# A vision tower on one core: edge products in row groups of 64, two pairs ahead, between the products of Q and K

## The chip, the cores and the metric

One core of a Trainium2 chip runs the whole kernel as one program. The metric is device time in microseconds. Before the change the median of three runs is 305.49 us (305.42 to 306.01).

## The reference, cut to what matters

Eight images of 3 x 256 x 256 go through three stages; the last two have weights of their own.

```python
def tok(x, scharr):                       # x (8, 3, 256, 256)
    gray = einsum('bchw,c->bhw', x, (0.2989, 0.587, 0.114))[:, None]
    edges = conv(gray, scharr, stride 1, 'SAME')          # two 3 x 3 filters
    return abs(edges).sum(axis=1) / 2     # (8, 256, 256): 256 tokens of width 256

def attn(x, Wq, bq, Wk, bk, Wv, bv, Wp):  # 16 heads of 16
    q, k, v = (x @ W + b for W, b in ...)
    q, k = q @ Wp, k @ Wp                 # for each head
    return softmax(q k^T / sqrt(16)) v

def ffn(x, ...):                          # 256 -> 1024 -> 256, weights dequantized
    h = layernorm(x) * gamma + beta
    return x + 0.5 * (silu(h @ w1 + b1) @ w2 + b2)

h = tok(x); h = h + attn(layernorm(h)); h = h + ffn(layernorm(h))
```

## The kernel before

Images are handled as four pairs. Each engine has its own list of instructions, run strictly in the order in which the code issues them; semaphores join them. There are three parts on the time axis: the image part with the products of Q, K and V (to about 100 us of the span), the attention loop (to about 207 us), and the MLP. Matrix products are split in a high and a low part of each operand, so one product of exact size takes three matmuls (`product`, line 1142).

**Image part.** For an image, ScalarE scales the first colour (`gray_scale`), VectorE adds the other two (`gray_add`, lines 724 and 725), ScalarE writes the high part (`gray_high`) and VectorE or GpSimd the low part (`gray_low`). The convolution is done on TensorE with band matrices: for a tile of 128 image rows (`t` is 0 or 1), and each of the two filters (`k`), nine matmuls (three column shifts `dx`, three high and low combinations) with 128 rows of contraction and 512 columns (two images of 256). A tenth (line 1164) adds what comes over the tile's edge, the halo, from 96 stacked rows. That is `tok(p, i)` with `i = 2 * t + k`. ScalarE takes the absolute value of each (line 1024, into `absd` or `hid`), VectorE adds the two (`edges`, line 794), and takes mean and variance (`tok_moments`); GpSimd computes `rstd` (line 543), VectorE normalises (line 813) into `xn`. TensorE transposes `xn` (`xt`), ScalarE and VectorE split it in `xt_h` and `xt_l`. Then come the six products of the pair, `qkv(p, 0)` to `qkv(p, 5)`: two of Q, two of K, one of V for each image. ScalarE (`qk_high`) and VectorE (`qkv_out`, line 838) take the first four out of PSUM, VectorE the last two.

**Order on TensorE** for pair `p`: `tok(p + 1, 0)` and `tok(p + 1, 1)`, the transposes of pair `p`, `tok(p + 1, 2)` and `tok(p + 1, 3)`, then the six products. They share the PSUM banks 4 to 7 by turns. In the last pairs the first ten heads' scores by query (line 1212) are put in between, by the table `HEAD_AT`; VectorE takes their largest value (`largest`, line 848).

**Way over DRAM.** Q and K go to DRAM and come back in another layout, both on SP's queue: `store_qk(p, i)` (line 379, two DMAs) once VectorE has read product `i`, and `load_qk(p, m, k)` (line 389, twelve DMAs for each half `m` of a pair). SP's order is: four stores of pair 0, 24 loads of pair 0, four stores of pair 1; then it waits until all edges are added, since the loads of pair 1 land where the image part has its buffers; twelve loads, the stores of pair 2, twelve loads, the stores of pair 3, and then the weights of the MLP (lines 401 and 404).

**Attention loop.** Slot `s` of 64 handles two heads: scores by query of slot `s + 10`, scores by key of slot `s` (lines 1235 and 1240, on partitions 0 to 47 and 64 to 111, into two banks), the exponential on ScalarE, the product with V (line 1260). In every fourth slot TensorE transposes the split maxima (`neg`, line 1270); for slot 11 that is `neg(2, 0)`. GpSimd's order there is: at slots 6, 7 and 8 the first steps of `w1_step` (dequantizing the MLP's first weights, lines 610 and 613, the first waits for the weights' DMA), at slot 9 `split_max(2, 0)` (lines 553 and 556), which `neg(2, 0)` waits for.

Of the kernel before, what the change touches and what calls it, by code (L numbers as in the profile page):

```python
# [5 lines left out]
def vit_tower_kernel(nc, x, scharr, Wq, bq, Wk, bk, Wv, bv, Wp, ln_gamma, ln_beta,  # L6
# [6 lines left out]
    fp32 = mybir.dt.float32  # L13
# [21 lines left out]
    HALF = P // 2  # L35
    NCOL = HALF + SPLIT
# [39 lines left out]
    halo_m = at("halo_m", 17.9375, [P, NT, 3], fp32)  # L76
    halo_p = at("halo_p", 18, [P, NT, 2, 3], fp32)
    halo_w = at("halo_w", 18.0625, [P, NT * 2], fp32)
    halo_wh = at("halo_wh", 18.125, [P, NT * 2], fp32r)
    halo_wl = at("halo_wl", 18.1875, [P, NT * 2], fp32)  # L80
# [16 lines left out]
    band_h = at("band_h", 83.25, [P, 2, 3, P], fp32r)  # L97
    band_l = at("band_l", 86.25, [P, 2, 3, P], fp32r)
    halo = at("halo", 89.25, [96, B, E], fp32r)
    halo_b = at("halo_b", 97.25, [96, NT, 2, P], fp32r)  # L100
# [11 lines left out]
    masks = at("masks", 141.25, [P, 3, P], fp32)  # L112
# [5 lines left out]
    halo_x = at("halo_x", 143, [32, B, E], fp32)  # L118
# [4 lines left out]
    bandp = at("bandp", 163, [P, 2, 3, P], fp32)  # L123
    band = at("band", 167, [P, 3, P], fp32)
    band1 = at("band1", 173, [P, 3, P], fp32)
# [28 lines left out]
    def norms_of(p):  # L154
        return (xt2_h, xt2_l) if p == PAIRS - 1 else (xt_h, xt_l)
# [6 lines left out]
    with ctx:  # L162
# [9 lines left out]
        s_halo = sem("halo_loaded")  # L172
# [14 lines left out]
        s_bandp = sem("second_band_parts_ready")  # L187
        s_band1 = sem("second_band_ready")
# [6 lines left out]
        s_wready = sem("qkv_weights_ready")  # L195
# [11 lines left out]
        s_fill = [sem(f"filled{r}") for r in range(4)]  # L207
        s_free = [sem(f"freed{r}") for r in range(4)]
# [32 lines left out]
        XT_LAST = (PAIRS - 2, 3)  # L241
        turns = []
        for p in range(-1, PAIRS):
            if p + 1 < PAIRS:
                turns.extend(("tok", p + 1, i) for i in range(2 if p >= 0 else 4))
            if p >= 0:
                if p + 1 < PAIRS:
                    turns.extend(("xt", p, kf) for kf in range(KE))
                    turns.extend(("tok", p + 1, i) for i in (2, 3))
                for i in range(6):  # L250
                    turns.append(("qkv", p, i))
                    if (p, i) == XT_LAST:
                        turns.extend(("xt", p + 1, kf) for kf in range(KE))
        turn = {key: n for n, key in enumerate(turns)}
        last_turns = [[key for key in turns if turn[key] % 4 == r][-1] for r in range(4)]

        def turn_bank(key):
            return bank[4 + turn[key] % 4]

        def wait_filled(eng, key):  # L260
            n = turn[key]
            eng.wait_ge(s_fill[n % 4], n // 4 + 1)

        def wait_freed(eng, key):
            n = turn[key]
            if n >= 4:
                eng.wait_ge(s_free[n % 4], n // 4)

        def wait_read(eng, key):
            n = turn[key]  # L270
            eng.wait_ge(s_free[n % 4], n // 4 + 1)

        def filled(key):
            return s_fill[turn[key] % 4]

        def freed(key):
            return s_free[turn[key] % 4]
# [4 lines left out]
        HEAD_AT = {("tok", 3, 1): 0, ("tok", 3, 3): 1, ("qkv", 2, 0): 2, ("qkv", 2, 2): 3, ("qkv", 2, 3): 4, ("qkv", 2, 5): 5,  # L282
# [74 lines left out]


# [5 lines left out]
        N3_READ = {n + 2: key for n, key in N3_MADE.items()}  # L364

# [3 lines left out]
        def _(eng):  # L369
# [37 lines left out]
            load_x(0)  # L407
            load_x(1)
# [5 lines left out]
            load_x(2)  # L414
            load_x(3)
# [6 lines left out]
            for b in range(4, B):  # L422
                load_x(b)
# [266 lines left out]
        def _(eng):  # L690
# [228 lines left out]
            for op in range(2):  # L919
                weights(op)  # L920
# [516 lines left out]
```

## Time and profile before

| | us |
|---|---|
| median of 3 runs | 305.49 |
| the profiled execution | 305.62 |
| its span | 303.9 |
| TensorE busy, of the span | 291.6 (96%) |
| VectorE busy | 214.6 (71%) |
| ScalarE busy | 161.5 (53%) |
| GpSimd busy | 130.9 (43%) |

The span runs from the first to the last instruction of the profiled execution; what lies around it is 1.7 us here. A busy share is an average over three parts with different limits. TensorE's matmuls overlap (a 512-column one shows 0.40 us, and the next starts 0.23 us later), so the distance between starts is what one costs.

### The profile page before, as it was taken

The page shows a single profiled execution, that of the slowest core. Times are in us where ns is not written, and L with a number is a line of the kernel's source. Part 1 is how long each engine was busy: PE and PEld are TensorE (multiplying, and loading weights), DVE is VectorE, ACT ScalarE, POOL GpSimd, SP SyncE. Part 2 cuts the span into 40 slices and gives each one's busy share as a digit, 9 for nine tenths or more (in the row PEclk, how much of TensorE's full clock was granted, in tenths as well). Part 3 has the DMA queues.
Part 4 walks back from the last instruction along what each step waited for, and adds up shares of the span by engine and source line. Part 5 has one row for each costly group of instructions (what it writes and reads, how often), then busy time and mean ns, then how long its engine had stood idle before and what let it go on. Part 6 is the DMA issues. An engine that isn't in the chain of part 4 may idle for free.

```text
span 303.9 us, 6265 instructions
## 1 busy us (share of the span) xinstructions
PE 291.6 (96%) x2328; PEld 229.6 (76%) x2328; DVE 214.6 (71%) x423; ACT 161.5 (53%) x304; POOL 130.9 (43%) x250
## 2 busy tenths in 40 slices
PE   6799999999999999999999999999999999999996
PEld 6678888887787666666666666667998998989976
DVE  8978994775899988888889887636845724633332
ACT  1492453433333577768776777867345343434550
POOL 7515250421100018862768572156769489500000
PEclk9999999999999999999999999999999999999999
DMA  6968028782497971778573000000000100200202
GB/s 211 327 195 275 1 92 284 208 287 101 125 296 220 331 279 54 189 175 280 156 186 77 4 3 0 2 0 2 0 3 13 59 0 0 71 0 0 71 0 69
DMA packets 26631, 35.30 MB, mean 116 GB/s; under 512 B 5082, under 2 KB 15594, under 8 KB 26602
## 3 DMA queue, kind: packets, MB, share of 16 engines
q1 hardware_dynamic: 26440, 34.77, 38.2%
q8 instruction: 18, 0.29, 0.4%
q10 hardware_dynamic: 162, 0.15, 0.2%
q14 instruction: 11, 0.09, 0.1%
HBM read 24.42 MB, written 10.49 MB: 115 GB/s over the span
## 4 chain that ended last, share of the span: by engine, by line
PE 66%; DVE 13%; SPq 8%; DMA 4%; ACT 4%; issue 3%; POOL 1%; ACTq 0%; DVEq 0%; POOLq 0%
PE bank L1142 39%; PE bank L1260 7%; PE bank L1212 6%; SPq L389 5%; PE bank L1235 3%; PE bank L1240 3%; SPq L379 3%; PE bank L1278 3%; DVE negmax L848 2%; DMA wscale<-in_L_ffn_fc_scales 2%; DVE gray L725 1%; PE bank L1164 1%; PE bank L1286 1%; ACT probs L1050 1%; PE bank L1270 1%
## 5 line engine op out<-in xcount | busy, mean ns | idle before, releaser
L848 DVE TENSOR_REDUCE negmax<-bank 128x2 f32<-128x512 f32 x128 | 82.1, 684 | 6.1 <-PE bank L1212 5.8
L1050 ACT ACTIVATE probs<-bank 128x512 f32<-128x512 f32 x128 | 66.3, 602 | 27.8 <-PE bank L1240 27.8
L902 DVE TENSOR_TENSOR y_l<-yf,y_h 128x512 fp32r<-128x512 f32 x32 | 24.2, 756 | 38.5 <-ACT yf L1076 38.4
L1073 ACT ACTIVATE y_h<-bank,b1col 128x512 fp32r<-128x512 f32 x32 | 22.0, 689 | 47.7 <-PE bank L1142 47.6
L1142 PE MATMUL bank<-w_h,y_h 128*128 128x256 f32 x128 | 36.9, 288 | 1.1 <-DVE y_l L902 0.7
L1142 PE MATMUL bank<-w_l,y_h 128*128 128x256 f32 x128 | 36.2, 283 | 0.0
L1142 PE MATMUL bank<-w_h,y_l 128*128 128x256 f32 x128 | 36.2, 283 | 0.0
L1260 PE MATMUL bank<-probs,vals 128*32 128x256 f32 x512 | 34.3, 385 | 0.0
L1212 PE MATMUL bank<-ks,qs 48*128 48x256 f32 x256 | 32.2, 329 | 1.3 <-DVE negmax L848 0.7
L1212 PEld LDWEIGHTS bank<-ks,qs 48*128 48x128 f32 x256 | 19.3, 184 | 15.6 <-DVE negmax L848 6.4
L1142 PEld LDWEIGHTS bank<-w_h,y_h 128*128 128x128 f32 x128 | 24.4, 190 | 2.9 <-DVE y_l L902 1.9
L1240 PEld LDWEIGHTS bank<-qs,ks 48*128 48x128 f32 x256 | 24.2, 185 | 2.7
L1235 PE MATMUL bank<-negrow,pick 48*128 48x512 f32 x128 | 26.0, 402 | 0.0
L1142 PE MATMUL bank<-nt_h,w_h 128*128 128x512 f32 x64 | 25.8, 402 | 0.0
L1240 PE MATMUL bank<-qs,ks 48*128 48x256 f32 x256 | 25.5, 277 | 0.0
L1142 PE MATMUL bank<-nt_h,w_l 128*128 128x512 f32 x64 | 25.3, 395 | 0.0
L1142 PEld LDWEIGHTS bank<-w_h,y_l 128*128 128x128 f32 x128 | 24.4, 191 | 0.7
L1142 PE MATMUL bank<-nt_l,w_h 128*128 128x512 f32 x64 | 24.9, 390 | 0.0
L1142 PEld LDWEIGHTS bank<-w_l,y_h 128*128 128x128 f32 x128 | 24.4, 191 | 0.0
L553 POOL TENSOR_SCALAR negsplit<-negmax 128x8 fp32r<-128x8 f32 x32 | 5.9, 205 | 38.4 <-DVE negmax L848 35.4
L563 POOL TENSOR_TENSOR hid<-hid,att 128x256 f32<-128x256 f32 x16 | 12.1, 755 | 22.9 <-DVE att L859 22.9
L1076 ACT ACTIVATE yf<-bank,b1col 128x512 f32<-128x512 f32 x32 | 21.8, 682 | 0.0
(147 smaller groups left out, 621.5 us busy)
## 6 DMA issues: line engine op xcount, KB each, us to landing
xr<-in_x SPq DMA_DIRECT2D x8, 768.0 KB, 9.4
qs<-qk_parts SPq DMA_DIRECT2D x48, 128.0 KB, 3.2
ks<-qk_parts SPq DMA_DIRECT2D x48, 128.0 KB, 3.4
qk_parts<-qk_h SPq DMA_DIRECT2D x16, 256.0 KB, 3.3
qk_parts<-qk_l SPq DMA_DIRECT2D x16, 256.0 KB, 3.5
wraw<-in_L_ffn_fc_q SPq DMA_DIRECT2D x4, 512.0 KB, 4.7
wscale<-in_L_ffn_fc_scales SPq DMA_DIRECT2D x4, 512.0 KB, 6.6
out<-osb SPq DMA_DIRECT2D x16, 128.0 KB, 1.8
```

Source lines behind the costliest of these rows:

```text
L389: eng.dma_start(dst[first:first + SPLIT - 2:3, r, m * 4:(m + 1) * 4, :].bitcast(fp32), src).then_inc(s_load[r][m], 16)
L563: eng.tensor_tensor(h, h, att[:, u % 2, :], ALU.add).then_inc(s_h2, 1)
L848: eng.tensor_reduce(negmax[:, b % 2, u, v], entry_bank(key)[:, :].rearrange("p (t k) -> p t k", t=NT), AX.X, ALU.max, negate=True).then_in ...
L902: eng.tensor_tensor(y_l[:, p % 2, f], yf[:, n % 2], y_h[:, p % 2, f].bitcast(fp32), ALU.subtract).then_inc(s_y, 1)
L1050: eng.activation(probs[:, n % PBUF], p2[n % 4][:, :], ACT.Exp).then_inc(s_exp, 1)
L1073: eng.activation(y_h[:, p % 2, f], src, ACT.Silu, bias=b1col[:, f:f + 1])
L1076: eng.activation(yf[:, n % 2], src, ACT.Silu, bias=b1col[:, f:f + 1]).then_inc(s_silu, 1)
L1142: ins = eng.matmul(dst, l, r, start=first and i == 0, stop=i == len(steps) - 1 and not more_after)
L1212: ins = eng.matmul(entry_bank(("head", k, v))[:, t * N:(t + 1) * N], qs[rows, r, u, c + t * P:c + (t + 1) * P], ks[rows, r, u, c:c + N], s ...
L1235: eng.matmul(p2[(n + v) % 4][:, :].rearrange("p (t n) -> p t n", t=NT), pick[rows, u % 4:u % 4 + 1].broadcast_to([SPLIT, P]), negrow[rows, ...
L1240: ins = eng.matmul(p2[(n + v) % 4][:, t * N:(t + 1) * N], ks[rows, r, u, c + t * P:c + (t + 1) * P], qs[rows, r, u, c:c + N], start=False, ...
L1260: ins = eng.matmul(av[OROWS * j:OROWS * (j + 1), 0:N], vals[:, b, t, h * VW:h * VW + OROWS], probs[:, (4 * G + j) % PBUF, t * N:(t + 1) * ...
```

## The change

- **Edges.** `tok(p, t)` handles both filters at once. The contraction is cut in two halves of 64 rows; the 128 output partitions are 64 rows of the one filter and 64 of the other. So there are nine pairs of matmuls, each of the pair on its own 64 partitions and into its own bank, and two halo matmuls (65 rows). ScalarE takes each bank with two activations of 64 partitions.
- **Bands.** Built in five steps on VectorE for both filters; GpSimd's share of it is gone.
- **Halo.** The border rows of each tile half are loaded once (24 rows for four images, six DMAs: the first group from ScalarE's queue, the second from SP's), turned to gray, split, and stacked with the three column shifts by three DMAs on SP's queue.
- **Order.** The edges of pairs 0 and 1 come before the products of pair 0; those of pair `p + 2` stand between the products of pair `p`, behind `qkv(p, 1)` and `qkv(p, 2)`. The transposes of pair `p + 1` stand behind `qkv(p, 3)`. The image part uses all eight banks for a while. The first two heads come later (`HEAD_AT`).
- **Who does what.** Normalising goes from VectorE to ScalarE (scale and bias; GpSimd computes the bias too), the high part of images 2 to 7 and V's weights go to GpSimd, the copies of the transposed weights from ScalarE to VectorE.
- **SP's order.** Images 0 to 3 first, then the weights of Q and K; the first halo stack and the second group's halo rows ahead of image 4.

The diff, cut to what the text speaks of:

```diff
-        XT_LAST = (PAIRS - 2, 3)
+        TOK_AT = (1, 2)
+        XT_AT = 3
+        turns = [("tok", p, i) for p in range(2) for i in range(4)] + [("xt", 0, kf) for kf in range(KE)]
...
-        HEAD_AT = {("tok", 3, 1): 0, ("tok", 3, 3): 1, ("qkv", 2, 0): 2, ("qkv", 2, 2): 3, ("qkv", 2, 3): 4, ("qkv", 2, 5): 5,
+        HEAD_AT = {("qkv", 1, 5): 0, ("qkv", 2, 0): 1, ("qkv", 2, 1): 2, ("qkv", 2, 2): 3, ("qkv", 2, 3): 4, ("qkv", 2, 5): 5,
...
+        def load_halo(eng, g):
+            for r in range(3):
+                for t in range(NT):
+                    first = 4 * (NT * r + t)
+                    row = (t * P + HALF - 1, t * P + HALF, P - t)[r]
+                    eng.dma_start(halo_x[first:first + 4, g], x[4 * g:4 * g + 4, :, row, :]).then_inc(s_halo_x, 16)
+
+        def stack_halo(eng, g):
+            eng.wait_ge(s_halo_l, g + 1)
+            for dx in range(3):
+                lo, hi = max(0, 1 - dx), E - max(0, dx - 1)
+                eng.dma_start(halo[dx:dx + 34:3, g, :, :, lo:hi].rearrange("r t b w -> r (t b) w").bitcast(fp32),
+                              halo_hl[:, g, lo + dx - 1:hi + dx - 1].bitcast(fp32)).then_inc(s_halo[g], 16)
...
-            load_x(0)
-            load_x(1)
+            for b in range(4):
+                load_x(b)
...
-            load_x(2)
-            load_x(3)
+            eng.wait_ge(s_border, 6)
+            stack_halo(eng, 0)
+            eng.wait_ge(s_halo_z, 2)
+            load_halo(eng, 1)
+            load_x(4)
             eng.dma_start(wv_src[:], Wv.rearrange("(k p) n -> p k n", p=P)).then_inc(s_wld, 16)
+            load_x(5)
...
+            stack_halo(eng, 1)
 
             for i in range(4):
                 store_qk(0, i)
...
@@ gpsimd: tok_rstd
+                eng.tensor_scalar(nmean_a[:, js], mv[:, js, 0], -1.0, 0.0, ALU.mult, ALU.add)
                 link(eng.tensor_scalar(vareps[:, js], mv[:, js, 1], EPS, 1.0, ALU.add, ALU.mult))
-                eng.tensor_tensor(rstd[:, js], vareps[:, js], mhalf[:, js], ALU.pow).then_inc(s_rstd, 1)
+                link(eng.tensor_tensor(rstd[:, js], vareps[:, js], mhalf[:, js], ALU.pow))
+                eng.tensor_tensor(shift_a[:, js], nmean_a[:, js], rstd[:, js], ALU.mult).then_inc(s_rstd, 1)
...
+            for b in range(2, 4):
+                gray_high(b)
+                gray_low(b)
+            eng.wait_ge(s_wld, 16 * (NT + 1))
+            link(eng.tensor_scalar(wqk_h[:, :, 2 * E:], wv_src[:], 1.0, 0.0, ALU.mult, ALU.add))
+            eng.tensor_tensor(wqk_l[:, :, 2 * E:], wv_src[:], wqk_h[:, :, 2 * E:].bitcast(fp32), ALU.subtract).then_inc(s_wvready, 1)
...
@@ vector: order
+            gray_add(0)
+            halo_add(0)
+            gray_low(0)
+            gray_add(1)
+            halo_low(0)
+            gray_low(1)
+            halo_bands()
+            gray_add(2)
+            gray_add(3)
+            for op in range(2):
+                eng.wait_ge(s_wt, op + 1)
+                eng.tensor_copy(wtr[:, op], bank[op][:, :]).then_inc(s_wtc, 1)
...
+            tok_stats(0, 0)
+            halo_add(1)
+            tok_stats(0, 1)
             for op in range(2):
                 weights(op)
+            halo_low(1)
+            gray_add(4)
+            for kf in range(KE):
+                xt_low(0, kf)
+            gray_add(5)
+            tok_stats(1, 0)
             for p in range(PAIRS):
                 for i in range(6):
                     qkv_out(p, i)
...
+                    if (p, i) == (0, 0):
+                        tok_stats(1, 1)
+                    if i in TOK_AT and p + 2 < PAIRS:
+                        if p == 0 and i == TOK_AT[1]:
+                            gray_add(6)
+                        tok_stats(p + 2, TOK_AT.index(i))
+                    if i == XT_AT and p + 1 < PAIRS:
                         for kf in range(KE):
                             xt_low(p + 1, kf)
...
@@ scalar
+            def edge(p, t):
+                for half in range(2):
+                    key = ("tok", p, 2 * t + half)
+                    rows = slice(HALF * half, HALF * (half + 1))
+                    wait_filled(eng, key)
+                    eng.activation(hid[rows, p, t].rearrange("p b e -> p (b e)"), turn_bank(key)[0:HALF, :], ACT.Abs)
+                    if p >= 1 and half == 0:
                         eng.wait_ge(s_edges, NT * (p - 1) + t + 1)
+                    eng.activation(absd[rows, t], turn_bank(key)[HALF:P, :], ACT.Abs).then_inc(freed(key), 1)
...
+            load_halo(eng, 0)
             gray_scale(0)
+            gray_high(0)
+            halo_scale(0)
             gray_scale(1)
...
+                    if i == 1 and p + 1 < PAIRS:
+                        for t in range(NT):
+                            tok_normalise(p + 1, t)
+                    if i in TOK_AT and p + 2 < PAIRS:
+                        edge(p + 2, TOK_AT.index(i))
...
@@ tensor: tok
+                for dx in range(3):
+                    for i, (w, g) in enumerate(((band_h, gray_h), (band_l, gray_h), (band_h, gray_l))):
+                        for half in range(2):
+                            rows = slice(HALF * half, HALF * (half + 1))
+                            eng.matmul(dst[half], w[rows, dx].rearrange("p k j -> p (k j)"), g[rows, p % 2, t, :, dx:dx + E],
+                                       start=dx == 0 and i == 0, stop=False)
```

## Rows read from the trace of the kernel before

**Rows 1.** The chain of waits, 77 to 119 us: start, duration, what
```profile
76.77 0.70 DVE hid L794
77.53 0.56 SPq L389
...
106.54 6.89 DMA wscale<-in_L_ffn_fc_scales
113.51 1.06 POOL w1full L610
```

**Rows 2.** Timelines of GpSimd and TensorE: start, us, engine, line [idle before <-releaser]
```profile
100.31 0.50 PE L1212 MATMUL bank<-ks,qs 48*128 48x256 f32 x4 [0.42 <-DVE negmax L848]
...
117.38 0.37 POOL L553 TENSOR_SCALAR negsplit<-negmax 128x8 fp32r<-128x8 f32 x2
...
118.34 0.40 PE L1270 MATMUL bank<-ident,negsplit 128*112 128x128 f32 x2 [0.30 <-POOL negsplit L556]
```

**Rows 3.** Timeline of SP's queue, 47 to 107 us
```profile
47.95 3.86 SPq L389 DMA_DIRECT2D qs<-qk_parts  x6
...
68.01 1.74 SPq L379 DMA_DIRECT2D qk_parts<-qk_l  x1
77.53 3.75 SPq L389 DMA_DIRECT2D qs<-qk_parts  x6
...
104.75 1.25 SPq L401 DMA_DIRECT2D wraw<-in_L_ffn_fc_q  x2
```

**Rows 4.** Timeline of TensorE: the edge products, and the first product of Q
```profile
13.90 0.47 PE L1142 MATMUL bank<-gray_h,band_h 128*128 128x512 f32 x1 [1.29 <-DVE gray_l L730]
...
16.97 0.40 PE L1142 MATMUL bank<-gray_h,band_h 128*128 128x512 f32 x1
...
19.10 0.39 PE L1164 MATMUL bank<-halo,halo_b 96*128 96x512 f32 x1
...
36.93 0.39 PE L1142 MATMUL bank<-xt_h,wqk_h 128*128 128x512 f32 x1
```

**Rows 5.** Timeline of TensorE: products on two groups of partitions
```profile
77.66 0.40 PE L1142 MATMUL bank<-xt_l,wqk_h 128*128 128x512 f32 x1
77.99 0.50 PE L1212 MATMUL bank<-ks,qs 48*128 48x256 f32 x4
...
109.47 0.40 PE L1235 MATMUL bank<-negrow,pick 48*128 48x512 f32 x2
...
109.71 0.40 PE L1240 MATMUL bank<-qs,ks 48*128 48x256 f32 x4
```

**Rows 6.** Timelines of ScalarE, VectorE and GpSimd in the image part
```profile
14.34 1.29 ACT L1012 ACTIVATE halo<-halo_x 32x512 fp32r<-32x512 f32 x2 [1.36 <-DMA halo_x<-in_x]
...
20.68 0.60 ACT L1024 ACTIVATE absd<-bank 128x512 f32<-128x512 f32 x1
...
25.29 0.68 DVE L794 TENSOR_TENSOR hid<-hid,absd 128x512 f32<-128x512 f32 x1
...
26.95 0.66 DVE L794 TENSOR_TENSOR hid<-hid,absd 128x512 f32<-128x512 f32 x1
...
36.77 0.69 DVE L725 SCALAR_TENSOR_TENSOR gray<-xr,gray 128x512 f32<-128x512 f32 x1
...
40.03 0.74 POOL L543 TENSOR_TENSOR rstd<-vareps,mhalf 128x2 f32<-128x2 f32 x1
...
41.51 1.47 DVE L725 SCALAR_TENSOR_TENSOR gray<-xr,gray 128x512 f32<-128x512 f32 x1
...
43.55 2.12 DVE L838 SCALAR_TENSOR_TENSOR qk_l<-bank,qk_bias,qk_h 128x512 fp32r<-128x512 f32 x3
```

**Rows 7.** Windows (busy us, instructions, by engine; granted clock) and waits (total, times, longest)
```profile
3.00:8.00 5.00, 5.00 (x26) 5.00 (x25) 4.71 (x21) 0.00 (x0) 3.75 (x14) 1.00 1.01 335
8.00:9.50 1.50, 1.50 (x17) 1.50 (x14) 1.23 (x9) 1.15 (x2) 1.50 (x5) 1.00 1.13 301
...
PE bank L1169 <- POOL ident L498: 2.7, 1, 2.7
```

More of the change, by code:

```diff
@@ L254, in vit_tower_kernel @@
-        turn = {key: n for n, key in enumerate(turns)}
-        last_turns = [[key for key in turns if turn[key] % 4 == r][-1] for r in range(4)]
+        TOK_AT = (1, 2)
+        XT_AT = 3
+        turns = [("tok", p, i) for p in range(2) for i in range(4)] + [("xt", 0, kf) for kf in range(KE)]
+        for p in range(PAIRS):
+            for i in range(6):
+                turns.append(("qkv", p, i))
+                if i in TOK_AT and p + 2 < PAIRS:
+                    turns.extend(("tok", p + 2, 2 * TOK_AT.index(i) + half) for half in range(2))
+                if i == XT_AT and p + 1 < PAIRS:
+                    turns.extend(("xt", p + 1, kf) for kf in range(KE))
@@ new lines, in vit_tower_kernel @@
+        turn = {key: n for n, key in enumerate(turns)}
+        fold_over, heads_begin = turn["qkv", 0, 0], turn["qkv", 1, 5]
+        turn_at, nth, uses = {}, {}, [[] for r in range(8)]
+        for n, key in enumerate(turns):
+            if fold_over <= n < heads_begin:
+                r = (0, 1, 2, 3, 6, 7, 4, 5)[(n - fold_over) % 8]
+            else:
+                r = 4 + (n if n < fold_over else n - heads_begin) % 4
+            turn_at[key], nth[key] = r, len(uses[r])
+            uses[r].append(key)
@@ L356, in wait_room @@
                     wait_drained(eng, last[0])
+            for r in sorted({ebank[key] for key in keys if not before[key]}):
+                wait_read(eng, uses[r][-1])
         LN_AT = (SLOTS - 32, SLOTS - 10)
@@ new lines, in _ @@
+            eng.memset(is_low[:], 1.0).then_inc(s_halom, 1)
+            eng.wait_ge(s_halom, 2)
+            for part in range(3):
+                eng.affine_select(out=halo_m[:], in_=halo_m[:], compare_op=ALU.not_equal, fill=1.0,
+                                  base=-12 * part, pattern=[[-3, 3], [-1, 3]], channel_multiplier=1).then_inc(s_halom, 1)
+                eng.wait_ge(s_halom, 3 + part)
+            link(eng.affine_select(out=is_low[:], in_=is_low[:], compare_op=ALU.is_ge, fill=0.0,
+                                   base=-12, pattern=[[0, 1]], channel_multiplier=1))
@@ L1143, in product, with tok @@
                 return ins
-            def tok(p, i):
-                t, k = i // 2, i % 2
-                key = ("tok", p, i)
-                wait_freed(eng, key)
-                if p == 0 and i == 1:
-                    eng.wait_ge(s_band1, 1)
-                if i == 0:
+            def tok(p, t):
+                keys = [("tok", p, 2 * t + half) for half in range(2)]
+                for key in keys:
+                    wait_freed(eng, key)
+                if t == 0:
                     if p == 0:
@@ L1325, in _ @@
             eng.wait_ge(s_ident, 1)
-            keep_busy(40, bank[0])
+            keep_busy(44, bank[0])
+            eng.wait_ge(s_gray, 2)
+            keep_busy(8, bank[0])
+            eng.wait_ge(s_band, 1)
+            eng.wait_ge(s_border, 6)
+            for t in range(NT):
+                tok(0, t)
             eng.wait_ge(s_wsrc, 32)
@@ L1333, in _ @@
                 ins.then_inc(s_wt, 1)
[L1334 to L1338 removed]
+            for t in range(NT):
+                tok_halo(0, t)
             eng.wait_ge(s_diag, 1)
```

443 lines of the change are left out of this document (191 added, 252 removed).

## The prediction

> **What bounds the kernel now.** I read the page's busy shares first: TensorE 96% of the span, VectorE 71%. That says "TensorE", and for most of the span it is true, but it does not say what a cheaper edge stage is worth. So the second view is the chain of waits, in order of time, between the last edge of the image part and the attention loop. From 77 to 118 us it does not run over TensorE at all [rows 1]: the last edge sum on VectorE (line 794, ends 77.47) releases SP's queue, SP issues copies until 104.75, then the MLP weights [rows 3], their DMA lands at 113.5, GpSimd dequantizes them, and only then does TensorE go on. The third view, the timeline around 118 us, shows the link to TensorE [rows 2]: `neg(2, 0)`, the twelfth slot's transpose, starts at 118.34 after an idle 0.30, released by GpSimd's `negsplit`, which stands behind three steps of `w1_step` in GpSimd's order. The fourth view, SP's timeline, gives the prices of the queue [rows 3]: the first load of `qs` at 47.95; pair 0's loads and pair 1's stores end at 69.75 (21.8 us without a gap); then a hole of 7.8 us, since `load_qk(1, 0, ..)` waits for all edges; then 77.53 to 104.75, 27.2 us of issue. So two chains tie at 118 us: TensorE's own work, and SP's queue with its hole.
>
> **TensorE's side.** In `tok` nine products of 512 columns and 128 rows take 16.97 to 19.10, 0.237 each [rows 4]. With the change each product has 64 rows and there is one for each half of the partitions. Do two such run at once? The attention loop has that form: two products of 512 columns on partitions 0 to 47 and 64 to 111 into two banks start at 109.47, and the next group starts at 109.71 [rows 5]. That is 0.24 for both, so I take 0.237 for a pair. Per `tok(p, t)`: before 2 x (2.13 + 0.24) = 4.7 us, after 2.13 + 2 x 0.24 = 2.6. Going from full products to row groups costs 0.10: 0.33 from 77.66 to 77.99 where 0.23 is usual [rows 5]. Twice per `tok`, 0.2; so 1.9 us are saved each time, 15 us in eight. By a sum of TensorE's work the kernel would win 15 us. I don't believe it, for the following. What comes out of PSUM grows: ScalarE needs four activations of 64 partitions for each edge sum where it needed two of 128, and one costs by its columns, 0.60 alone [rows 6]: 1.0 us more per sum, 8 in all, on an engine with room for them, but in a row that VectorE waits for. The Trainium skill says the same in "TensorEngine Tiling (Array Packing)", "PSUM Bottleneck": tiling speeds up TensorE and not the emptying of PSUM; if that were the bound throughout, 8 of the 15 us would go.
>
> **The start, to `qkv(0, 0)`.** Before, `tok(0, 0)` starts at 13.90 and `qkv(0, 0)` at 36.93 [rows 4]. Now ScalarE scales image 1 only after the halo's gray, and so after the halo's rows have landed. Before, ScalarE got them at 14.34 [rows 6]. Now it issues them 0.8 us earlier and half as many rows, so I take 11 (between 7.4, the end of their issue if each takes the 0.7 us it takes before, and 14.3). From there: scale, two adds, high and low parts of image 1 by turns on ScalarE and VectorE, some 4.8 us: `tok(0, 0)` starts at 15.8, 1.9 later. The bands are cheaper on VectorE (five steps of 384 elements, and none late), the twelve small copies into `halo_b` take about what is saved. The two `tok` then take 4.4 us for the 9.9 before, but the rest is not TensorE's: VectorE does images 2 and 3 and the two copies of the transposed weights first, the fold ends near 25.5, ScalarE now has four activations per edge sum instead of two, the halo of the second group is waited for on VectorE ahead of `tok_stats(0, 1)`, and GpSimd has V's weights ahead of the first `rstd`. Laid end to end this gives the transposes of pair 0 at about 34 and `qkv(0, 0)` at 36.5, 0.4 earlier. Bounds: 34.5 (wv and image 4 early) and 38.5 (each hand-over 0.1 us dearer).
>
> **The step that decides: the last read of pair 0's products.** SP stores four products of Q and K and only then loads any. Before, nothing stood between those products and VectorE read the last at 45.67 (line 838, 43.55 + 2.12), 8.7 us after `qkv(0, 0)` began; the loads began 2.3 us behind it [rows 3, 6]. Afterwards VectorE has between its last `xt_low` and that read: two `gray_add` (two steps of 0.69 each, 1.4), four `tok_stats` (1.66 each, the distance of 25.29 and 26.95), four `qkv_out` (0.69 each): 2.8 + 6.6 + 2.8 = 12.2 us [rows 6]. And it waits once: `tok_stats(2, 0)` needs ScalarE's edges of pair 2, which stand behind `tok_normalise(1, 1)`, behind `rstd` of pair 1 on GpSimd. That is GpSimd's four small steps (the power alone 0.74; I take 1.7), the normalising that has moved to ScalarE (0.7), and four activations of 0.5 (they take 0.60 one by one, and follow each other a tenth closer), less what VectorE does meanwhile: 4.1 us. So the read is at 36.5 + 12.2 + 4.1 = 52.8. Bounds: 48.5, by TensorE alone (four products, two `tok`, one hand-over), and 55.5 (start at 38.5, and `gray_add` 0.8 dearer where GpSimd's subtraction holds it up). SP is free for the loads about 1.8 us later, the third store no longer being piled up before the fourth: 54.6, for 47.95.
>
> **From there to the attention loop.** The edges are all done by 69, so the hole of 7.8 us is gone, but it has been eaten: 54.6 + 21.8 = 76.4, then 27.2, and 0.4 for loads right behind 2 MB of stores: SP reaches the MLP weights at 104.0, against 104.75. From that issue to TensorE's `neg(2, 0)` it is 13.6 us [rows 1, 2]: 117.6, for 118.3. TensorE itself comes to the loop earlier. Before it is 63.4 us from `qkv(0, 0)` to 100.31 [rows 2, 4]; four `tok` go from 4.7 to 2.8, -7.8, and some 3 us of waits come in (`xt_low(1)` on VectorE 2.1, the gray of later pairs twice 0.9, less those of before); so 36.5 + 63.4 - 7.8 + 3 = 95. Its twelfth slot would be due 18 us later, at 113, and there it waits some 4.5 us for GpSimd. Behind that point the code is the same and every engine stands where it stood, 0.7 us earlier. The other edits (banks 0 to 3 used too, `xt2` by turns, the first two heads later) are covered by that wait and I cost them at nothing; without that cover they show in the loop's start alone.
>
> **The number.** 0.7 us earlier: a span of 303.2 for 303.9; the profiled execution took 305.62, 1.7 more than its span, so 304.9; the median before is 305.49, 0.13 less: **304.8 us**.
>
> **Rivals.** (a) *TensorE's clock falls in the wait before slot 12*; this one ends slower. Before, the longest wait of TensorE is 2.7 us, at the very start [rows 7]. The warm-up transposes show a slow and a fast pace: 26 in 5.0 us (192 ns each), then 17 in 1.5 us (88 ns), although the granted clock reads 1.00 in both [rows 7]. If a wait of 4.5 us brings the slow pace back for as long, half of up to 5 us is lost, 1.7 to 2.7 us, and the loop, TensorE being its bound, gives none back: 304.8 + 2.2 = 307.0. It decides if the wait is one piece and longer than any the kernel has now. Against it: the wait may be 3 us only. The Trainium skill, in "TensorE: Matmul & The Clock Gate", "What's actually happening", says that an idle TensorE is gated to 1.2 GHz and gets 2.4 GHz back only after sustained work; no row of this trace shows such a fall.
> (b) *SP's chain is shorter than I think*, because the last read of pair 0 comes near its lower bound: loads from 50.5 on, slot 12 at 113.5 to 114: 4.5 us less, 301. Beyond 5.3 less TensorE is the bound again. For it: ScalarE has idle time in this stretch.
> (c) *A slower start*: the halo lands at 14 or the second group's rows are late. Each us there moves the loads one for one; from 55.3 on the change loses. Two more: 306.9.
> (d) *Two halves don't run at once*: the products cost what they did plus the switches, `tok` sits between Q's and K's products, loads later by 7, TensorE at the loop by 106: 311. Against it speak the pairs in the loop [rows 5].
>
> **Chances.** Forecast 0.48, (a) 0.27, (b) 0.12, (c) 0.09, (d) 0.04. A run can tell 0.2% (0.6 us) from no change. The forecast's own spread is 1.5 us either way (303.3 to 306.3), of which half is faster, three tenths same: 0.24, 0.14, 0.10. With (b) faster is 0.37, and a small part of (a), where the loads are early, makes it 0.41; same 0.19; slower 0.40. The range reaches from the middle of (b) to the dear end of (a): 301.5 to 308.5.
>
> **What would show it.** In SP's timeline the first `qs` load near 54.6 and no hole before `load_qk(1, 0, ..)`; the MLP weights' issue near 104. In TensorE's timeline pairs of half products every 0.24 us; `tok(0, 0)` at 15.8, `qkv(0, 0)` at 36.5, the loop from 95 on, and one wait of 4 to 5 us before `neg(2, 0)` at 117.6, released by `negsplit`. (a) is right if the products behind that wait come at twice the distance, (b) if the loads start before 52. The forecast is wrong in kind if no such wait is there and the time has fallen by 5 us or more.

## The result, and the profile after

| | us |
|---|---|
| before, median of 4 runs beside it | 305.46 (305.32 to 306.01) |
| after, median of 4 runs | 315.31 (314.17 to 317.39) |
| ratio | 1.0327, 95% interval 1.0268 to 1.0386 |
| the profiled execution after, and its span | 317.39, 315.6 |

The change makes the kernel 3.3% slower. I had forecast 304.8, and no rival reached 315. Below, one execution of E1 (342.36 us) and two of the kernel before (310.6 and 310.37) ran in a slower state, at a lower granted clock, and are left out of every median, range and ratio.

The page of the kernel after, busy shares and two rows of the forty slices (busy tenths of TensorE, and its granted clock):

```profile
PE 284.4 (90%) x2332; PEld 221.0 (70%) x2332; DVE 206.3 (65%) x415; ACT 173.8 (55%) x330; POOL 136.9 (43%) x268
...
PE   5599059889699998899999999999999999999996
...
PEclk9989759999999999599999999999999999999999
```

TensorE has 7 us less to do (284.4 for 291.6) and the span is 11.7 us longer. A zero stands in the fifth slice of TensorE's row, about 32 to 40 us, and right behind it the clock reads 0.5. TensorE's waits say who it is (line waited at, releaser: total, times, longest):

```profile
PE bank L1244 <- ACT xn L1083: 9.6, 1, 9.6
PE bank L1234 <- DVE gray L784: 3.8, 1, 3.8
PE bank L1234 <- POOL ident L546: 3.6, 1, 3.6
PE bank L1198 <- DVE vals L892: 3.1, 1, 3.1
PE bank L1198 <- DVE xt_l L882: 3.0, 2, 1.5
PE bank L1337 <- POOL negsplit L610: 1.9, 1, 1.9
```

One wait of 9.6 us, ahead of the transposes of pair 0. ScalarE's `xn` is only its last link; the chain of waits (start, duration, what) goes further back:

```profile
23.76 8.62 DMA bv<-in_L_attn_bv
32.38 0.08 issue
32.46 0.63 POOL wqk_h L701
...
33.16 1.26 POOL wqk_l L702
...
34.92 0.72 POOL rstd L596
```

And GpSimd's own timeline shows the place:

```profile
32.46 0.62 POOL L701 TENSOR_SCALAR wqk_h<-wv_src 128x512 fp32r<-128x512 f32 x1 [8.38 <-DMA bv<-in_L_attn_bv]
...
37.30 0.19 POOL L597 TENSOR_TENSOR shift_a<-nmean_a,rstd 128x2 f32<-128x2 f32 x1
```

GpSimd waits 8.4 us before it splits V's weights, and behind that wait, in its order, stands the first `tok_rstd`. The wait is for three transfers (`wait_ge(s_wld, 16 * (NT + 1))`), V's weights and the bias `bv` twice; SP issues `bv` at 23.2, behind images 4 and 5, and it has landed at 32.4. The mean and variance of pair 0's first row tile had been ready at 27.1, so 5.3 us of the wait hold up pair 0. V's two instructions take 2.0 more. Behind them ScalarE, whose order is as strict, writes the halo's high part and takes the edges of pair 1's first row tile out of PSUM (37.06 to 40.34) between its two parts of `xn`, although the second `shift_a` is ready at 37.5. Everything of pair 0 stands behind: `rstd`, `xn`, the transposes at 41.60, the first product of Q at 45.04, where 36.93 was [rows 4].

What TensorE does after the wait is slow too (timeline of TensorE, then windows: start and end, length, the busy time of each engine with its instructions in brackets, and behind the last bracket the granted clock, 0.50 being the lower of its two levels, 1.2 GHz):

```profile
41.60 1.94 PE L1244 MATMUL bank<-ident,xn 128*128 128x128 f32 x8 [9.62 <-ACT xn L1083]
45.04 0.76 PE L1198 MATMUL bank<-xt_h,wqk_h 128*128 128x512 f32 x1 [1.50 <-DVE xt_l L882]
...
46.03 0.63 PE L1198 MATMUL bank<-xt_l,wqk_h 128*128 128x512 f32 x1
46.46 0.63 PE L1198 MATMUL bank<-xt_h,wqk_h 128*128 128x512 f32 x1
...
48.91 0.39 PE L1198 MATMUL bank<-xt_h,wqk_h 128*128 128x512 f32 x1
49.14 0.39 PE L1198 MATMUL bank<-xt_h,wqk_l 128*128 128x512 f32 x1
```

```profile
16.00:20.00 4.00, 4.00 (x28) 3.08 (x28) 3.76 (x22) 0.53 (x1) 0.94 (x3) 0.74 0.29 79
36.00:40.00 4.00, 0.00 (x0) 0.00 (x0) 1.80 (x3) 3.89 (x8) 1.39 (x5) 0.50 0.21 46
...
44.00:48.00 4.00, 2.96 (x7) 2.41 (x8) 3.63 (x9) 2.94 (x6) 1.61 (x2) 0.50 0.01 2
...
128.00:132.00 4.00, 4.00 (x29) 3.13 (x31) 2.18 (x5) 1.86 (x5) 2.96 (x4) 0.50 0.04 10
```

Until 48.6 a product starts 0.43 behind the one before, then 0.23. The first window is an earlier and smaller fall: TensorE waits 3.8 us for the first gray, and the first edge products start 0.43 apart until 18.1. The last window is a fall in the attention loop; it stands behind the wait before `neg(2, 0)` (timelines of TensorE and GpSimd):

```profile
124.40 1.07 PE L1327 MATMUL bank<-probs,vals 128*32 128x256 f32 x16
127.40 0.65 PE L1337 MATMUL bank<-ident,negsplit 128*112 128x128 f32 x2 [1.93 <-POOL negsplit L610]
...
129.42 0.63 PE L1302 MATMUL bank<-negrow,pick 48*128 48x512 f32 x2
129.85 0.63 PE L1307 MATMUL bank<-qs,ks 48*128 48x256 f32 x4
...
134.38 0.39 PE L1279 MATMUL bank<-ks,qs 48*128 48x256 f32 x2
```

```profile
122.59 1.05 POOL L664 TENSOR_SCALAR w1full<-wraw 128x1024 f32<-128x1024 int32 x1 [4.76 <-DMA wscale<-in_L_ffn_fc_scales]
```

SP's timeline holds the two rows the forecast was built on, the first load of `qs` and the MLP's weights:

```profile
63.38 3.84 SPq L427 DMA_DIRECT2D qs<-qk_parts  x6
...
112.90 1.28 SPq L439 DMA_DIRECT2D wraw<-in_L_ffn_fc_q  x2
```

### The profile page after: what moved, and what is told of

It is laid out like the page before. It is cut to its first block, busy times and chain, and to the rows that moved or that the text cites. A ratio compares the mean times of both kernels' runs of the same rounds, so it can differ in the third digit from the quotient of the medians.

```text
span 315.6 us, 6328 instructions
## 1 busy us (share of the span) xinstructions
PE 284.4 (90%) x2332; PEld 221.0 (70%) x2332; DVE 206.3 (65%) x415; ACT 173.8 (55%) x330; POOL 136.9 (43%) x268
## 4 chain that ended last, share of the span: by engine, by line
PE 57%; DVE 9%; DMA 8%; ACT 7%; SPq 7%; POOL 5%; issue 4%; ACTq 1%; DVEq 0%; POOLq 0%
PE bank L1198 30%; PE bank L1327 7%; PE bank L1279 6%; PE bank L1302 4%; PE bank L1307 3%; PE bank L1345 3%; DMA bv<-in_L_attn_bv 3%; DVE negmax L909 3%; DMA wscale<-in_L_ffn_fc_scales 2%; SPq L427 2%; DMA halo_x<-in_x 2%; SPq L417 2%; PE bank L1216 1%; ACT xn L1083 1%; PE bank L1337 1%
## 5 line engine op out<-in xcount | busy, mean ns | idle before, releaser
L1327 PE MATMUL bank<-probs,vals 128*32 128x256 f32 x512 | 35.1, 393 | 0.0
L1307 PEld LDWEIGHTS bank<-qs,ks 48*128 48x128 f32 x256 | 24.9, 189 | 2.7
L1100 ACT ACTIVATE qk_h<-bank,qk_bias 128x512 fp32r<-128x512 f32 x16 | 11.0, 687 | 19.9 <-PE bank L1198 18.1
```

What stands on the lines that cost most here:

```text
L1100: eng.activation(qk_h[:, i], turn_bank(key)[:, :], ACT.Identity, bias=qk_bias[:, op, m:m + 1]).then_inc(s_hi, 1)
L1307: ins = eng.matmul(p2[(n + v) % 4][:, t * N:(t + 1) * N], ks[rows, r, u, c + t * P:c + (t + 1) * P], qs[rows, r, u, c:c + N], start=False, ...
L1327: ins = eng.matmul(av[OROWS * j:OROWS * (j + 1), 0:N], vals[:, b, t, h * VW:h * VW + OROWS], probs[:, (4 * G + j) % PBUF, t * N:(t + 1) * ...
```

## The experiments

Eleven kernels ran. The ratio is to the kernel before on the same chip; its median was 305.79 beside E1 to E4, 305.64 beside E5 to E8 and 306.38 (305.42 to 309.85) beside E9 to E11. Each of these groups ran on a chip of its own, so a difference between runs of two groups is rougher than one inside a group.

| | edit | median (range), us | ratio, 95% interval |
|---|---|---|---|
| E1 | V's weights behind the first `rstd` | 308.86 (307.18 to 310.87) | 1.0103, 1.0045 to 1.0161 |
| E2 | `w1_step` from slot 10 | 314.62 (312.74 to 315.56) | 1.0280, 1.0239 to 1.0321 |
| E3 | both | 308.33 (308.0 to 308.6) | 1.0079, 1.0056 to 1.0103 |
| E4 | the two halves one after the other | 319.89 (318.81 to 320.52) | 1.0457, 1.0428 to 1.0485 |
| E5 | E1, banks shifted by a turn | 307.62 (306.46 to 308.7) | 1.0063, 1.0025 to 1.0102 |
| E6 | E5, spare transposes in the early waits | 307.24 (305.77 to 309.36) | 1.0057, 1.0008 to 1.0105 |
| E7 | E6, `w1_step` from slot 10 | 304.20 (303.69 to 304.7) | 0.9952, 0.9926 to 0.9978 |
| E8 | the kernel after, spare transposes alone | 313.97 (313.03 to 315.59) | 1.0277, 1.0239 to 1.0315 |
| E9 | the kernel *before*, `w1_step` from slot 10 | 305.15 (305.02 to 305.34) | 0.9950, 0.9926 to 0.9974 |
| E10 | E5, `w1_step` from slot 10 | 306.10 (304.51 to 306.94) | 0.9973, 0.9948 to 0.9997 |
| E11 | E7, halves one after the other | 308.83 (308.66 to 309.04) | 1.0056, 1.0027 to 1.0086 |

### E1: V's weights behind the first rstd

```diff
@@ gpsimd
+            for t in range(NT):
+                tok_rstd(0, t)
             eng.wait_ge(s_wld, 16 * (NT + 1))
             link(eng.tensor_scalar(wqk_h[:, :, 2 * E:], wv_src[:], 1.0, 0.0, ALU.mult, ALU.add))
             ...
-            for t in range(NT):
-                tok_rstd(0, t)
```

> Changed kernel, with V's weights split on GpSimd behind the two rstd of pair 0 instead of ahead of them. Theory A (the start is late because GpSimd waits for the broadcast of bv, 8.4 us, ahead of rstd(0, t)): the transposes of pair 0 move from 41.6 to about 34 us of the span, TensorE's clock doesn't fall between 35 and 48 us, the first load of qs moves from 63.4 to 54 to 55, and neg(2, 0) from 127.4 to 117 or 118; median 305 to 308 for the changed kernel's 315.3. Rival B (ScalarE's edges and the second halo group's loads are what the start waits for, the bv wait only lies beside them): transposes at 39 or later, 313 to 315.

Waits of TensorE, and the first load of `qs` and the MLP's weights on SP's queue:

```profile
PE bank L1198 <- DVE vals L892: 3.1, 1, 3.1
PE bank L1244 <- ACT xn L1083: 2.4, 1, 2.4
```

```profile
56.28 3.83 SPq L427 DMA_DIRECT2D qs<-qk_parts  x6
...
105.02 1.26 SPq L439 DMA_DIRECT2D wraw<-in_L_ffn_fc_q  x2
```

The wait of 9.6 is 2.4 now, the transposes of pair 0 start at 34.36 for 41.60, and the first load comes 7.1 us earlier, so the cause of the late start is shown. The time falls by 6.5 us in the median, to 0.9 above theory A's range, and stays above the kernel before: something else costs too. Against theory A TensorE's clock still falls: the window from 36 to 40 us is at 0.50 here as well, behind waits of 2.4 and 1.9 us. And in front of `qkv(1, 5)`, the last product of pair 1, stands a wait of 3.1 that the kernel before doesn't have.

### E2 and E3: the MLP's first weights later in GpSimd's order

```diff
@@ gpsimd: w1_step
-            spare = [s for s in range(6, SLOTS - 8) if s % 8 in (0, 2, 3, 4, 6, 7)]
+            spare = [s for s in range(10, SLOTS - 8) if s % 8 in (0, 2, 3, 4, 6, 7)]
```

> Changed kernel, with the first step of w1_step at slot 10 of the attention loop instead of 6, so that split_max(2, 0) no longer stands behind the wait for the MLP's weights. Theory A (the wait ahead of neg(2, 0) and the fall of the clock behind it come from SP's chain through GpSimd): neg(2, 0) starts 2 us earlier with no wait, the clock stays at 1.00 from 127 to 134 us, 5 us less: about 310. Rival C (the clock falls there for another reason, or the wait moves to the next neg): within 1.5 us of 315.3.

The wait before `neg(2, 0)` is gone in E2 and the loop runs at full clock, as theory A has it, but the median is only 0.7 us lower, which is rival C's number; the ranges overlap. TensorE reaches that transpose at 126.87. In the kernel after it had been ready for it at 125.5 and was released at 127.40. The difference lies in the image part: in E2's profile the clock falls behind the wait of 3.1 for `vals`, and that costs 1.2 us. In the profile of the kernel after, the same wait has no fall behind it (E2 first, then the kernel after; the granted clock is 0.64 and 1.00):

```profile
80.00:84.00 4.00, 2.57 (x12) 2.57 (x12) 1.34 (x3) 0.00 (x0) 0.27 (x2) 0.64 0.93 316
80.00:84.00 4.00, 2.72 (x19) 2.36 (x20) 2.15 (x6) 0.00 (x0) 0.20 (x1) 1.00 0.93 317
```

Six kernels have this wait of 3.1 us. The profiles of five (E1 to E4 and E8) show a fall behind it; that of the kernel after doesn't. Its absence there looks like chance, and that E2's edit brought the fall out isn't shown. Over the whole span the mean granted clock of E2's four executions (0.962 to 0.973) is no higher than that of the kernel after (0.961 to 0.973).

> Both edits of the two runs before together. Theory A: the start 7.7 us earlier plus the clock's loss there, and SP's chain out of the way of the attention loop, so that the loop is set by TensorE's and VectorE's own work: loop from 95 to 97 us, median 300 to 303, faster than the kernel before the change (305.5). Rival D (the two gains are the same microseconds, since both lie ahead of the same slot): not below the better of the two single edits, 305 or more.

E3 is 0.5 us below E1 in the median, within the spread of E1's runs, and far from theory A's 300 to 303; rival D's number came. In E1 TensorE comes to `neg(2, 0)` at 119.78 and no longer waits there, so there was little left for the second edit to gain. The start is worth most, the MLP step something only when TensorE comes early enough to meet it.

### E4: do two halves run at once?

```diff
@@ tensor: tok
-                for dx in range(3):
-                    for i, (w, g) in enumerate(...):
-                        for half in range(2):
+                for half in range(2):
+                    for dx in range(3):
+                        for i, (w, g) in enumerate(...):
```

> Changed kernel, with the nine products of the upper 64 partitions issued first and then the nine of the lower, so that no two neighbours can run side by side. If neighbours on different partition groups share TensorE's time, each tok(p, t) costs 2.1 us more, 17 us in all. Theory A (TensorE is not what sets the image part of this kernel; it waits there for 20 us and more): only part of it reaches the end, the two tok of pair 2 and the two of pair 3 that stand between the products, 4 to 9 us. Rival E (TensorE's work sets the time): 15 us or more. If there is no side by side at all: no difference.

4.6 us slower than the kernel after, TensorE busy 294.8 for 284.4. In the kernel after, the timeline shows two products to a row and 0.24 from row to row at full clock, with 0.34 at the first for the change of form:

```profile
25.96 0.50 PE L1216 MATMUL bank<-gray_h,band_h 64*128 64x512 f32 x2
26.30 0.40 PE L1216 MATMUL bank<-gray_h,band_l 64*128 64x512 f32 x2
26.54 0.39 PE L1216 MATMUL bank<-gray_l,band_h 64*128 64x512 f32 x2
```

So rival (d) is out, and the row pairs do what was costed.

### E5: the bank that comes up twice

The wait of 3.1 us in E1 and in the kernel after:

```profile
81.28 0.39 PE L1198 MATMUL bank<-wqk_h,xt_h 128*128 128x256 f32 x1 [3.06 <-DVE vals L892]
```

`qkv(1, 4)` is the last turn in the order over eight banks, and gets bank 4; `qkv(1, 5)` is the first in the order over four, and gets bank 4 again. TensorE has to wait until VectorE, late itself, has read the product just written. One turn more in the second order takes the clash away:

```diff
-                r = 4 + (n if n < fold_over else n - heads_begin) % 4
+                r = 4 + (n if n < fold_over else n - heads_begin + 1) % 4
```

> As the first run (V's weights behind rstd of pair 0), and the turn of PSUM banks from qkv(1, 5) on begins with bank 5 instead of bank 4, which qkv(1, 4) has just filled. Theory F (TensorE's wait of 3.1 us ahead of qkv(1, 5), and the clock's fall behind it, come from two neighbours in the order sharing bank 4, so that TensorE waits until VectorE has read the first): no such wait, clock 1.00 from 74 to 80 us, 3 to 5 us less than the first run's 309.9, so 305 to 307. Rival G (the first head's scores are late anyway, since pair 0's loads of q and k have just landed): the wait moves behind qkv(1, 5), less than 1 us.

The wait for `vals` is gone, and the clock is at 1.00 from 74 to 80 us. The median, expected at 305 to 307, is 1.2 us below E1's, on another chip and with ranges that overlap, so what this edit is worth in time isn't shown. What TensorE gained it loses in part to the next thing in the row, SP's queue by way of GpSimd:

```profile
120.88 0.40 PE L1337 MATMUL bank<-ident,negsplit 128*112 128x128 f32 x2 [2.10 <-POOL negsplit L610]
```

### E6, E7, E8 and E10: the clock, and what it hides

```diff
@@ tensor (E6, E7)
-            keep_busy(44, bank[0])
+            keep_busy(78, bank[0])
...
+            keep_busy(22, bank[1])
             for kf in range(KE):
                 xt(0, kf)
+            keep_busy(12, bank[1])
             eng.wait_ge(s_wready, 4)
```

`keep_busy(n, ..)` is the kernel's own helper, n transposes of the identity into a bank that isn't in use. E8 has 84 and 12 of them at the two lower places, in the kernel after, and nothing else.

> Changed kernel with 84 transposes of the identity ahead of the transposes of pair 0 and 12 ahead of qkv(0, 0), nothing else: TensorE's wait of 9.6 us is the same wait, filled with work of no use. It tells the clock's price at the start from the wait's. Theory A: clock 1.00 from 36 to 48 us, qkv(0, 0) ends 1.5 us earlier, the first load of qs 2 to 3 us earlier than 63.4, median 312 to 313.5 for 315.3. If the clock costs nothing there: 315.

In E8's profile the clock stays at 1.00 from 32 to 48 us, the products of pair 0 come every 0.23, and the first load of `qs` is at 62.11, 1.3 us earlier (2 to 3 were expected). That is what the fall at 36 to 48 us cost. The median falls by 1.3 too, with ranges that overlap. The profiled execution is the slowest of the four, at the lowest granted clock (0.978 for 0.984 to 0.989), and in it the clock also falls at two other places: behind a wait of 1.9 us for `xt_l` (0.65 from 64 to 68), and behind the bank clash (0.56), where it didn't in the profile of the kernel after:

```profile
80.00:84.00 4.00, 2.91 (x14) 2.69 (x14) 1.00 (x3) 0.00 (x0) 0.01 (x1) 0.56 1.05 390
```

> As the run before, with TensorE kept busy by transposes of the identity where it waits: 78 instead of 44 at the very start, 22 ahead of the transposes of pair 0, 12 ahead of qkv(0, 0). Theory H (what is left of the loss at the start is the clock): granted clock 1.00 in the whole image part, tok(0, 0) at full pace, another 1 to 3 us less: 303 to 305. Rival I (the waits themselves cost, not the clock): within 1 us of the run before.

> As the run before, with the first w1_step at slot 10 instead of 6. If SP's chain (first load of qs plus 62.6 us) is again what neg(2, 0) waits for, this takes 1 to 4 us more off: 301 to 303. If TensorE reaches slot 11 no earlier than GpSimd, no difference.

E6 is level with E5 in time, as rival I said, and theory H's clock came only in part: it is at 1.00 up to 56 us, and then falls behind a wait of 1.9 us for `xt_l` (0.67 from 56 to 60). E7 has the same wait in the same place and no fall. In E6's profile TensorE is 2.3 us earlier at `neg(2, 0)` (118.57) than in E5's profile, waits 1.89 there, and the clock falls behind that wait (0.72 from 120 to 124), so the next `neg` is at 126.98. Not all of the 2.3 comes from the spare transposes: the first load is at 55.66 in E6, 57.87 in E5, and 56.47 in E10, which has E5's code up to there. E7 takes the wait away, and 3.0 us with it, with ranges apart; 304.20 is still above the 301 to 303 expected. E6's window, and the clock's row of E7's page, which has no fall at all:

```profile
56.00:60.00 4.00, 4.00 (x12) 2.85 (x12) 3.31 (x7) 0.69 (x1) 2.40 (x3) 0.67 0.76 237
...
PEclk9999999999999999999999999999999999999999
```

> The changed kernel with three edits: V's weights behind the first rstd, banks 4 to 7 shifted by one turn, w1_step from slot 10; no transposes added. It takes the added transposes out of the best variant (304.20). Theory 'the MLP step was the price, the clock a second one': against the variant without the late w1_step (307.62) the wait of 2.1 us before neg(2, 0) goes, and with it nothing more: 305.0 to 306.0; the best variant's last 1 to 1.5 us are the clock's in the first 50 us. Rival 'the clock decides alone': TensorE's earlier falls delay the edges and so SP's queue, and the time stays at 307 or more. Rival 'the transposes do nothing': 304.2.

E10 without the spare transposes is at 306.10, 0.1 above the first theory's range; E7 and E10 ran on different chips, so of the 1.9 us between them I take only the sign. Its windows show the clock at 0.67 from 16 to 20 and 0.50 from 36 to 40.

### E9: whose gain is it?

```diff
@@ gpsimd: w1_step, in the kernel before
-            spare = [s for s in range(6, SLOTS - 8) if s % 8 in (0, 2, 3, 4, 6, 7)]
+            spare = [s for s in range(10, SLOTS - 8) if s % 8 in (0, 2, 3, 4, 6, 7)]
```

> The kernel before with one edit: the first steps of w1_step stand from slot 10 on instead of from slot 6, so neg(2, 0) no longer waits for the MLP weights' DMA. It asks whose gain the 0.5% of the best variant is. Theory 'the gain belongs to the changed image part': before, neg(2, 0) waits only 0.30 us, TensorE is busy 96% of the span and its clock is 1.00, so the edit is worth 0 to 0.3 us here: 305.2 to 305.8, ratio 0.999 to 1.001. Rival 'the gain is that of the MLP step alone, which the order of the kernel before had needed as well': 304.2 to 304.8, ratio 0.996 to 0.998.

Half open: by its time it is just below the first theory's range, by its ratio below even the rival's. `neg(2, 0)` is at 117.78 for 118.34, 0.6 us earlier [rows 2], and 305.15 is 0.3 below the fastest run of the kernel before on that chip, but 1.2 below its median there, which is 0.6 to 0.7 higher than in the earlier groups. So 0.3 to 1.2 us of the 1.4 that E7 gains may come from this one line, which the kernel before could have without the change. By medians that leaves 0.2 to 1.1 us for the change itself, mended in three places; by the ratios, 0.9952 for E7 and 0.9950 for E9, it leaves nothing. No run compares the two on one chip, so no gain of the change is shown.

### E11: what the row pairs are worth at full clock

The edit is that of E4, made in E7.

> The best variant (304.20) with the loop of tok turned: all 18 products of half 0 first, then all of half 1, so no two of different halves stand next to each other; what is computed is the same. In this variant the clock is 1.00 throughout, so the price of the edges' TensorE time is read without the clock. By TensorE's sum eight tok cost 2.1 us more each. Theory 'the image part is set by the row of hand-overs, of which TensorE's part is the first four tok': the first four tok stand before the products of pair 0 (4 x 2.1 = 8.4, of which half lies under VectorE's gray steps), and tok(2, 0) and tok(2, 1) before the last read: 4 to 8 us more, 308 to 312. Rival 'row pairs save nothing beside other engines' work, the kernel is set by VectorE throughout': 304 to 306. Rival 'TensorE's time counts in full': 17 us more, 321.

4.6 us more than E7, in the range of the first theory (on another chip; the kernel before differs by 0.7 between them). But the range was hit with a wrong term in its working, so in part by luck. (Each `tok` has nine products for each half, not the 18 that the text above says.) TensorE's timeline of one `tok`:

```profile
45.13 0.39 PE L1216 MATMUL bank<-gray_l,band_h 64*128 64x512 f32 x1
45.14 0.62 PE L1216 MATMUL bank<-gray_h,band_h 64*128 64x512 f32 x2
45.48 0.51 PE L1216 MATMUL bank<-gray_h,band_l 64*128 64x512 f32 x2
45.72 0.51 PE L1216 MATMUL bank<-gray_l,band_h 64*128 64x512 f32 x2
45.95 0.40 PE L1216 MATMUL bank<-gray_h,band_h 64*128 64x512 f32 x1
```

Six products of half 0 stand alone, then three rows with two each, then six of half 1 alone: the halves overlap although they aren't neighbours in the order, the first three of half 1 running beside the last three of half 0. So `tok` takes 15 steps, not 18, and standing apart costs 1.3 us each (43.85 to 48.02 for 41.88 to 44.75 in E7), some 10 in eight, where I had written 17. TensorE's busy time is 10.4 higher in E4 than in the kernel after and 8.7 higher in E11 than in E7. Of these 10 us some 4.6 reach the end; TensorE waits 2.1 us less for `xt_l` and 0.8 less for `negmax` in E11 than in E7, which is part of what the rest runs into.

## Why the prediction was wrong, step by step

**The sum of the error.** In the profiled execution: the first load of `qs` came 8.8 us later than forecast (63.38 for 54.6); from there to the MLP's weights 49.5 us, forecast 49.4; from the weights to `neg(2, 0)` 14.5, forecast 13.6; behind it the fall of the clock in the attention loop, 127.40 to 134.38 = 6.98 us, where the same slots take 118.34 to 122.60 = 4.26 before (its last row below): 2.7. 8.8 + 0.1 + 0.9 + 2.7 = 12.5, and 317.39 is 12.5 above 304.9. It is the slowest of the four; the median misses by 10.5.

```profile
122.60 0.50 PE L1212 MATMUL bank<-ks,qs 48*128 48x256 f32 x4
```

**The start: wrong, and it is the step that failed.** "GpSimd has V's weights ahead of the first `rstd`" stands in the forecast, laid end to end at what the two instructions cost. The same sentence had to name what these wait for. I had the diff with SP's order before me: `bv` behind image 4 and V's weights, image 5 in between. In the first part of the start the forecast was close (the first edge product at 16.25 for 15.8). The transposes of pair 0 came at 41.60 for about 34 and the first product of Q at 45.04 for 36.5, far above the bound of 38.5, because that bound allowed for hand-overs and not for a transfer. 5.3 us of this are the wait for `bv` beyond the time at which pair 0's mean and variance were ready; the rest is ScalarE's order behind it and the slow clock. With V's weights behind (E1) the transposes are at 34.36 and the first product of Q at 37.87, inside the bounds. Rival (c) had the right kind of price, each us of the start moving the loads one for one, but it looked at the halo.

**The last read of pair 0's products: right within 1 us.** 17.3 us behind the first product of Q (62.4 less 45.04), forecast 16.3, and the first products ran at the slow pace, which was not in the forecast. VectorE's wait for pair 2's edges is 4.5 us, forecast 4.1. SP's loads follow 1.0 us behind the read's end, forecast 1.8.

**SP's queue: right.** No hole, 49.5 us. The idea that this queue, and not TensorE, sets when slot 12 begins held in the kernel after, in E5 and in E6, where TensorE waits for it: 64.0, 63.0 and 62.9 us join the first load to `neg(2, 0)`, forecast 63.0. With only the start mended (E1) it no longer holds: 56.28 + 63.0 = 119.3, and TensorE comes at 119.78 without a wait.

**TensorE at the loop: wrong, and only E7 shows it.** Forecast was 95, from 36.5, 58.5 us for the way, and therefore 4.5 us of slack before `neg(2, 0)`. In E7, at full clock and without clash, the way takes 37.59 to 99.45, 61.9 us. The saving of 1.9 per `tok` is there (41.88 to 44.75, 2.9 for 4.7). The waits on the way, which I took to add 3 us, are 6.0 for 1.3 before, so they add 4.7; the rest of the 3.3 us by which the way is longer than forecast stays open. The last three waits stand here, in E7's timeline of TensorE:

```profile
95.88 0.40 PE L1337 MATMUL bank<-ident,negsplit 128*112 128x128 f32 x2 [0.72 <-POOL negsplit L610]
96.87 0.51 PE L1279 MATMUL bank<-ks,qs 48*128 48x256 f32 x4 [0.58 <-DVE negmax L909]
...
99.45 0.51 PE L1279 MATMUL bank<-ks,qs 48*128 48x256 f32 x4 [0.46 <-DVE negmax L909]
```

I put them down to an edit that I had costed at nothing, though no run moves it back: the first two heads come later, so the same ten heads' maxima stand closer together on VectorE, 89% busy from 90 to 100 us, and TensorE waits for them. Where the cover of 4.5 us was to be, there were about 2 us (E5: 2.1, E6: 1.9).

**The bank turns: wrong.** Costed at nothing under the same cover, they hold a wait of 3.1 us and, in the profiles of E1 to E4 and E8, a fall of the clock behind it. The clash can be read off the diff: two orders of banks meet at `heads_begin`, and the last number of one is the first of the other.

**Rival (a), the clock: right in kind, wrong in its condition.** The fall behind the wait before `neg(2, 0)` cost 2.7 us, the top of its bounds. But it was to come only behind a wait longer than any the kernel had, 2.7 us, and it came behind one of 1.93; that it struck in the place I had named is in part luck. It also came in places I hadn't named, behind waits of 3.8 and 9.6 us in the kernel after and behind 3.1 us in five others. The sentence of the Trainium skill that I set against the trace of before ("TensorE: Matmul & The Clock Gate", "What's actually happening": an idle TensorE is gated to 1.2 GHz and gets the higher level back only after sustained work) is borne out by the windows at 0.50 and by products 0.43 apart until 48.6. The Trainium skill's other sentence, in "TensorEngine Tiling (Array Packing)", "PSUM Bottleneck", says that tiling speeds up TensorE and not the emptying of PSUM; the runs agree as far as only 4.6 of some 10 us reach the end, but none separates the emptying from the other engines' work.

**Rival (b): not met.** Its condition, the last read near the lower bound, never came about; even in E7 the first load is at 55.94. Why the first load is no earlier there, with the first product of Q at 37.59, is VectorE's and ScalarE's row of steps as forecast: 37.59 + 16.3 + 1.8 = 55.7.

## What to carry to other kernels

Read for every wait in the new order what it counts, and which of the transfers it counts is issued last: a wait for "the weights" that also counts a bias stands or falls with the bias (V's weights alone had landed at 27.7, 4.7 us before `bv`). Cost nothing at zero under a cover before that cover has itself been added up with the same care as the forecast; here the 4.5 us were assumed, and three small edits leant on them. And where an engine's speed depends on its being busy, a wait can cost more than its length, by 1.2 to 2.7 us here, and what taking one away is worth depends on which others are left: E1, the bank turn, the transposes and the MLP step brought 6.5, 1.2, 0.4 and 3.0 us in the median in that order (the middle two within the spread), where the MLP step alone brought 0.7.

## What the runs showed of the hardware

- Waits of 2 to 4 us brought TensorE's granted clock down to 0.50 in some of these runs (E1: windows 36 to 40 and 76 to 78 us), and it depends on more than the wait's length: behind the same wait of 3.1 us the clock stayed at 1.00 in the kernel after and fell in E1 to E4 and E8; behind the same wait of 1.9 us for `xt_l` it fell in E6 and E8 and stayed at 1.00 in E7.
- Transposes of the identity hold it up: in E8, with them in the wait of 9.6 us, the clock is at 1.00 from 32 to 48 us, where it is at 0.50 from 36 to 48 without them.
- A small transfer can be late: `bv`, a bias row spread over the partitions, was issued at 23.2 and had landed 8.6 us after its issue ended, while images were being loaded on the same queue; V's weights, issued 1.1 us earlier, took 5.1.
- Products on the two halves of the partitions overlap without being neighbours in TensorE's order: three of nine did in E11, each beside one that stands three places ahead of it (starts 45.14 and 45.37, in a row of products 0.23 apart).
- An activation of 64 partitions and 512 columns takes 0.59 us, as one of 128 does [rows 6]; four of them in a row are 0.60 apart, where the forecast had 0.5.
